# One unit's similarities two images ahead, behind the cluster sums, in a clustering and convolution kernel

## The chip, the cores and the metric

The kernel runs on one core of one Trainium2 chip. The metric is the device time of one execution in microseconds (us). The engines are named TensorE (PE), its weight loads (PEld), VectorE (DVE), ScalarE (ACT), GpSimd (POOL) and SyncE (SP), which issues the transfers.

## What is computed

Input x is 8 images of 512 channels by 32 x 48 pixels, float32; there are 40 centroids and a 512 x 512 weight matrix.

```python
xn = x / jnp.maximum(jnp.linalg.norm(x, axis=1, keepdims=True), EPS)
cn = centroids / jnp.maximum(jnp.linalg.norm(centroids, axis=1, keepdims=True), EPS)
sim = jnp.einsum('bchw,nc->bnhw', xn, cn)
idx = jnp.argmax(sim, axis=1)
onehot = jax.nn.one_hot(idx, N, dtype=x.dtype)
sum_x = jnp.einsum('bhwn,bchw->bnc', onehot, x)
count = jnp.sum(onehot, axis=(1, 2))
centroids_local = sum_x / jnp.maximum(count, 1.0)[..., None]
gathered = centroids_local[jnp.arange(B)[:, None, None], idx]
delta = jnp.transpose(gathered, (0, 3, 1, 2)) - x
alpha = jnp.exp(-jnp.mean(delta * delta, axis=1, keepdims=True))
y = x + alpha * delta
out = jnp.einsum('oc,bchw->bohw', W, y) + b[None, :, None, None]
return jax.nn.relu(out)
```

The pixel's own norm doesn't change its argmax, so the kernel leaves it out.

## The kernel before

**Units and slots.** An image has 1536 pixels, cut into three units of 512; unit g is part g % 3 of image g // 3, and there are 24. Channels lie on partitions in 4 chunks of 128. The order of all work is written out by hand, one list for each engine; engines meet at semaphores only. From unit 3 on the lists are loops over g, and I call one turn of the loop a slot. A slot holds two strands:

- *The unit itself.* TensorE's `gather(g, h)` multiplies the one-hot by the image's centroid means G, two of the four chunks for each half h, into the PSUM tile `gat`. VectorE's `delta` subtracts x into Z; ScalarE's `square` and VectorE's `add_squares` (three adds), ScalarE's `move_upper`, VectorE's `fold`, ScalarE's `high_sum` and VectorE's `low_sum` make the squared length in two parts, which TensorE's `sum_squares` adds over partitions into `al`. In the slot behind it ScalarE makes `exp`, VectorE `scale`s Z by it, GpSimd's `y_half` adds x, ScalarE's `high_half` rounds y to its high part YH and GpSimd's `low_half` makes the rest YL. Two slots after its gather (LAG = 2) comes `convolve(g, o)`: for each of four output groups o, 12 matmuls (4 chunks x YH, YL with the high weights and YH with the low ones) into one of two banks of `main`, then ScalarE's `relu`. A group waits until the relu two groups before it has emptied its bank, and group 0 waits for the halves of YL as it comes to them.
- *The next image.* Its similarities (`similarities`, L846, output tile 64 rows wide, two side by side) stand behind `gather(g, 1)`: units 0 and 1 in the first slot of an image, unit 2 in the second. ScalarE's `copy_sims` takes them out; `transpose_sims`, then VectorE's `best_sims` and `first_best` make the one-hot in the second slot. In the third slot `sum_clusters` (L891, also 64 rows wide) sums x by cluster for all three units, then `gather(g, 1)` and one convolution group follow, then `add_halves` (L901, L902), for which ScalarE's `copy_sums` and VectorE's `low_clusters` come first; `scale_means`, `high_means`, `rest_of_mean` and `parts_of_mean` (L449) make G for the gathers of the next slot. `count_onehot` counts the pixels of a cluster on ScalarE and writes a copy into `simS`.

**Pixels on partitions.** `sum_clusters` needs x turned. SyncE loads each unit a second time in blocks, and VectorE's `transpose_half` (L393) turns it into XT, two halves a unit; units 4 and 5 are turned by TensorE (`turn`) and copied by ScalarE (`keep_turned`). From unit 7 on, the first two units of an image are split in three bf16 parts: GpSimd's `first_rest` (L354, 2048 elements) and VectorE's `second_rest` (L401, 2048 elements, both of its inputs in SBUF) make the rests in XR.

**x itself** has two buffers. `load_x(g)` waits until `y_half` of unit g - 6 is made.

**The queue of a slot's end.** In slot order VectorE's list ends with `second_rest(g + 3)` in an image's first and second slot. GpSimd's list is, for each unit, `y_half` twice, `low_half` twice, then `first_rest` if a unit is due.

**Before the loop** the units 0 to 2 have lists of their own. There GpSimd's `add_chunks` (L362, L365) adds the squares of a unit in three adds, in place of the steps above, `sum_squares_direct` (L938) sums them, and unit 0's first two convolution groups are made in passes (`high_passes`, then L1058 with the low half of y).

Of the kernel before, what the change touches and what calls it, by code (L numbers as in the profile page):

```python
# [14 lines left out]
P = 128  # L15
# [14 lines left out]
NK = P  # L30
# [9 lines left out]

TURNED = (PARTS + 1, PARTS + 2)

# [6 lines left out]
def y_on_vector(g, h):  # L49

    return g == 0 or (g == 1 or g >= TAIL) and h == 1

# [42 lines left out]
def build(nc, x, cent, w, bias, out):  # L95
# [3 lines left out]
    with ctx:  # L99
# [58 lines left out]
        simP = [fa[:, 0, 0:256], fa[:, 1, 0:256], fa[:, 0, 256:512]]  # L158
# [53 lines left out]
        def squares(g, h):  # L212
            if g < DIRECT:

                return (OUT[0][:, :, :], OUT[1][:, :, :], XR[:, 0, :, :])[g][:, pair(h), :]
            return SQ[:, :, :] if h == 0 else gat[:, :, :]

# [95 lines left out]
        def _(pool):  # L313
# [66 lines left out]
        def _(dve):  # L380
# [71 lines left out]
            def delta(g, h):  # L452
                dve.wait_ge(gat_done, 2 * g + h + 1)
                if g >= 2:
                    wait_low(dve, g - 2, h)
                v_.tensor_tensor(Z[g % 2][:, pair(h), :], banks(g, h)[:, :, :],  # L456
                                 X[g // PARTS % 2][:, pair(h), span(g)], ALU.subtract).then_inc(z_done, 1)

# [95 lines left out]
            parts_of_mean(1)  # L554
            transpose_half(6, 0)
            low_half(1, 1)
            transpose_half(6, 1)
            for g in range(PARTS, UNITS):
                b, p = divmod(g, PARTS)
                beside = b + 1 < BATCH  # L560
                delta(g, 0)
                scale(g - 1, 0)
                scale(g - 1, 1)
                delta(g, 1)
# [3 lines left out]
                if beside and p == 2:  # L568
                    low_clusters(b + 1)
# [28 lines left out]
        def _(act):  # L598
# [7 lines left out]
            def keep_turned(g, half):  # L606

                done = PARTS * 2 + 2 * TURNED.index(g) + half + 1
                act.wait_ge(xp_done, done)
                a_.activation(XT[:, g % PARTS, HALF * half:HALF * (half + 1), :], (gat, main)[half][:, :, :],  # L610
                              ACT.Copy).then_inc(xe_act, 1)
# [501 lines left out]
```

## Time and profile before

| what | us |
|---|---|
| median of 3 runs | 414.45 |
| lowest, highest | 414.08, 415.33 |
| the profiled execution's own time | 414.81 |
| its span (first to last instruction) | 413.0 |
| TensorE busy | 405.5 |
| VectorE busy | 330.2 |
| ScalarE busy | 258.1 |
| GpSimd busy | 267.8 |

All rows come from one profiled execution. Starts are us from the span's start. A row with x2 merges two instructions.
### The profile page before, as it was taken

The numbers are of one execution on the slowest core, as the hardware profiler recorded it, in microseconds if no ns is written. First come the engines' busy times: TensorE is split into PE (matmuls) and PEld (weight loads), VectorE is DVE, ScalarE is ACT, GpSimd is POOL, SyncE is SP. The second block draws the span as 40 slices with busy tenths as digits, with TensorE's granted clock in tenths as the row PEclk, the third lists the DMA queues.
The fourth block names the chain that finished last, engine by engine and source line by source line (L and its number), as shares of the span: only waits on it lengthen the run. The fifth ranks groups of instructions, "written<-read, shape, count | busy, mean of one in ns | idle before, by whom it ended". The sixth has DMA issues, their size and how long they took to land.

```text
span 413.0 us, 5757 instructions
## 1 busy us (share of the span) xinstructions
PE 405.5 (98%) x2080; PEld 289.5 (70%) x2085; DVE 330.2 (80%) x404; ACT 258.1 (62%) x354; POOL 267.8 (65%) x120
## 2 busy tenths in 40 slices
PE   9999999999999999999999999999999999999996
PEld 6746475875777767775867757776777758777885
DVE  2438986689889889899798888898798996898730
ACT  6566773766674775665855676656846657576542
POOL 2003886993699666993879946996769937433420
PEclk9999999999999999999999999999999999999999
DMA  7992497767589395966979575993966240222223
GB/s 263 374 243 54 94 250 202 195 214 144 201 231 280 102 252 164 273 168 178 267 183 237 192 160 188 255 252 119 254 158 220 104 140 2 102 102 103 102 81 124
DMA packets 77823, 74.59 MB, mean 181 GB/s; under 512 B 13716, under 2 KB 52628, under 8 KB 77796
## 3 DMA queue, kind: packets, MB, share of 16 engines
q1 hardware_dynamic: 77796, 74.23, 64.7%
q8 instruction: 17, 0.28, 0.3%
q14 instruction: 10, 0.08, 0.1%
HBM read 46.30 MB, written 25.17 MB: 173 GB/s over the span
## 4 chain that ended last, share of the span: by engine, by line
PE 91%; POOL 4%; ACT 2%; DVE 1%; issue 1%; ACTq 0%; POOLq 0%
PE main L949 21%; PE main L950 20%; PE main L951 20%; PE fa L846 10%; PE sump L891 8%; PE gat L927 5%; POOL yl L347 2%; PE fa L855 1%; PE al L933 1%; PE al L984 1%; POOL xr L362 1%; PE main L964 1%; POOL o L362 1%; PE gat L964 1%; POOL o L365 1%; PE main L1058 1%
## 5 line engine op out<-in xcount | busy, mean ns | idle before, releaser
L949 PE MATMUL main<-yh,wh 128*128 128x512 f32 x376 | 153.3, 408 | 0.0
L950 PE MATMUL main<-yl,wh 128*128 128x512 f32 x376 | 146.7, 390 | 0.0
L951 PE MATMUL main<-yh,wl 128*128 128x512 f32 x376 | 146.6, 390 | 0.0
L340 POOL TENSOR_TENSOR z<-z,x 128x1024 f32<-128x1024 f32 x41 | 98.6, 2424 | 63.9 <-DVE z L480 63.9
L347 POOL TENSOR_TENSOR yl<-z,yh 128x1024 fp32r<-128x1024 f32 x43 | 103.8, 2434 | 9.1 <-ACT yh L639 9.1
L647 ACT ACTIVATE o<-main,bcol 128x512 f32<-128x512 f32 x96 | 65.6, 684 | 61.3 <-PE main L951 60.5
L949 PEld LDWEIGHTS main<-yh,wh 128*128 128x128 f32 x376 | 70.6, 188 | 21.3 <-issue 4.6
L951 PEld LDWEIGHTS main<-yh,wl 128*128 128x128 f32 x376 | 70.6, 188 | 15.1
L950 PEld LDWEIGHTS main<-yl,wh 128*128 128x128 f32 x376 | 70.7, 188 | 14.0
L354 POOL TENSOR_TENSOR xr<-xt 128x2048 f32<-128x2048 f32 x11 | 51.5, 4682 | 18.2 <-DVE xt L393 18.2
L456 DVE TENSOR_TENSOR z<-gat,x 128x1024 f32<-128x1024 f32 x46 | 56.0, 1218 | 6.8 <-PE gat L927 6.6
L480 DVE TENSOR_TENSOR z<-z,al 128x1024 f32<-128x1024 f32 x48 | 56.3, 1214 | 3.9 <-ACT al L634 3.9
L639 ACT ACTIVATE yh<-z 128x1024 fp32r<-128x1024 f32 x48 | 50.6, 1053 | 4.5 <-POOL z L340 2.9
L846 PE MATMUL fa<-x,c_t 128*64 128x256 f32 x384 | 46.9, 394 | 0.0
L393 DVE STREAM_TRANSPOSE xt<-xs 128x1024 f32<-128x1024 f32 x38 | 46.4, 1230 | 0.0
L846 PEld LDWEIGHTS fa<-x,c_t 128*64 128x64 f32 x384 | 26.6, 140 | 18.4 <-issue 7.0
L621 ACT ACTIVATE sq<-z 128x1024 f32<-128x1024 f32 x21 | 22.3, 1061 | 26.9 <-DVE z L456 26.9
L401 DVE TENSOR_TENSOR xr<-xr 128x2048 bf16<-128x2048 f32 x11 | 36.0, 3275 | 0.2
L621 ACT ACTIVATE gat<-z 128x1024 f32<-128x1024 f32 x21 | 21.5, 1024 | 21.3 <-DVE z L456 21.3
L891 PE MATMUL sump<-xt,oh 128*64 128x512 f32 (+1 forms) x148 | 31.7, 537 | 0.0
L362 POOL TENSOR_TENSOR o<-o 128x512 f32<-128x512 f32 x4 | 5.1, 1284 | 36.2 <-ACT o L621 36.2
L927 PE MATMUL gat<-oht,g 128*128 128x512 bf16 x87 | 26.7, 384 | 0.8 <-DVE g L449 0.4
(130 smaller groups left out, 394.2 us busy)
## 6 DMA issues: line engine op xcount, KB each, us to landing
out<-o SPq DMA_DIRECT2D x23, 1024.0 KB, 6.3
x<-x SPq DMA_DIRECT2D x21, 1024.0 KB, 5.5
xs<-x SPq DMA_DIRECT2D x76, 256.0 KB, 5.4
x<-x SPq DMA_DIRECT2D x12, 256.0 KB, 5.1
o<-w SPq DMA_DIRECT2D x1, 1024.0 KB, 8.9
out<-o SPq DMA_DIRECT2D x4, 256.0 KB, 2.0
sq<-centroids SPq DMA_DIRECT2D x2, 80.0 KB
oht<-oh SPq DMA_TRANSPOSE x7, 3.7
```

The costliest lines, as they stand in the source:

```text
L340: pool.tensor_tensor(z, z, X[g // PARTS % 2][:, pair(h), span(g)], ALU.add).then_inc(y_pool, 1)
L347: pool.tensor_tensor(YL[g % 2][:, pair(h), :], Z[g % 2][:, pair(h), :], YH[g % 2][:, pair(h), :].bitcast(F32), ALU.subtract).then_inc(lo_p ...
L354: pool.tensor_tensor(XR[:, g % PARTS, :, :].rearrange("p t c -> p (t c)"), xt.rearrange("p t c -> p (t c)"), halfword(xt, 1), ALU.subtract ...
L456: v_.tensor_tensor(Z[g % 2][:, pair(h), :], banks(g, h)[:, :, :], X[g // PARTS % 2][:, pair(h), span(g)], ALU.subtract).then_inc(z_done, 1)
L480: v_.tensor_tensor(z, z, al[:, :].unsqueeze(1).to_broadcast([P, 2, UNIT]), ALU.mult).then_inc(za_done, 1)
L639: a_.activation(YH[g % 2][:, pair(h), :], Z[g % 2][:, pair(h), :], ACT.Copy).then_inc(hi_done, 1)
L647: a_.activation(OUT[g % 2][:, o, :], main[:, o % 2, :], ACT.Relu, bias=bcol[:, o:o + 1]).then_inc(relu_done, 1)
L846: last = t_.matmul(simP[u][NPAD * h:NPAD * (h + 1), :], cT[:, k, :], toks, start=(k == 0), stop=(k == KC - 1))
L891: last = t_.matmul(sumP[NPAD * h:NPAD * (h + 1), :], onehot[:, slot(u, tile), :], x_part[:, tile * C:(tile + 1) * C], start=(opens and t = ...
L949: t_.matmul(main[:, o % 2, :], WH[:, k, rows], YH[g % 2][:, k, :], start=(k == 0), stop=False)
L950: t_.matmul(main[:, o % 2, :], WH[:, k, rows], YL[g % 2][:, k, :], start=False, stop=False)
L951: last = t_.matmul(main[:, o % 2, :], WL[:, k, rows], YH[g % 2][:, k, :], start=False, stop=(k == KC - 1))
```

## The change

1. From image 3 on, one unit's similarities are made two images ahead: in the third slot of an image b, directly behind the cluster sums of image b + 1, come those of unit 0 of image b + 2. The other two units' follow together in the second slot. The places of the three in PSUM are exchanged so that unit 0's does not lie where the mean is made. This holds in the slots of units 5, 8, 11, 14 and 17 (`late_group`); the slot of unit 20 stays as it was.
2. In those slots `add_halves` goes ahead of `gather(g, 1)`, and the slot's last convolution group and `sum_squares(g)` go behind the first gather of the next slot. ScalarE's copies, means and relus are put in an order that goes with it.
3. VectorE: in those slots `low_clusters` comes after the scaling, a transposed half on either side of `delta(g, 1)`, G before `low_sum`, and `second_rest(g + 4)` at the end, which stood in the next slot. `second_rest` is two instructions of 1024 instead of one of 2048.
4. GpSimd: for the unit handled in those slots `first_rest` goes ahead of the two `low_half`.
5. At the start: one tile of unit 4 is turned ahead of the similarities; the squares of unit 2 are added by VectorE; the low passes of unit 0 are made half by half; unit 6's second transposed half goes into slot 3.
6. `count_onehot` writes in place.

The list of SyncE, with all transfers, is the same in both kernels.

TensorE, the slot of unit 8, from its first gather. Before (L933 is the sum of squares of unit 7, L891 the cluster sums):

```order
L933 MATMUL al<-shl,ones 128x512
L927 MATMUL gat<-oht,g 128x512 x2
L891 MATMUL sump<-xt,oh 64x512 x6
...
L891 MATMUL sump<-xr,oh 64x512 x4
L927 MATMUL gat<-oht,g 128x512 x2
L949 MATMUL main<-yh,wh 128x512
```

And after (L953 the cluster sums, L908 similarities, L963 and L964 `add_halves`, L991 `gather`):

```order
L991 MATMUL gat<-oht,g 128x512 x2
L953 MATMUL sump<-xt,oh 64x512 x6
...
L953 MATMUL sump<-xr,oh 64x512 x4
L908 MATMUL fa<-x,c_t 64x256 x8
L963 MATMUL fa<-sums_h,select 128x512
L964 MATMUL fa<-sums_l,select 128x512
L991 MATMUL gat<-oht,g 128x512 x2
L1013 MATMUL main<-yh,wh 128x512
```

One unit's similarities and the two matmuls of `add_halves` now stand between the sums and the second gather.

VectorE, the slot of unit 8, from `low_clusters` (L435) to the next slot's first `delta` (L456). Before (L393 is the transpose, L474 `low_sum`, L449 G):

```order
L435 TENSOR_TENSOR sums_l<-sump,sums_h 128x512
L428 TENSOR_SCALAR cols<-cols 128x1
...
L466 TENSOR_TENSOR al<-sq,gat 128x512
L470 TENSOR_TENSOR al<-upper_sum,al 64x512
L441 SCALAR_TENSOR_TENSOR fa<-part,cols,fa 128x512
L444 CAST part<-fa 128x512
L474 TENSOR_TENSOR shl<-al,shl 64x512
L449 SCALAR_TENSOR_TENSOR g<-part,cols,fa 128x512
L393 STREAM_TRANSPOSE xt<-xs 128x8x4x32 x2
L456 TENSOR_TENSOR z<-gat,x 128x1024
```

And after (L456 is now `low_clusters`, L414 the transpose, L477 `delta`, L504 `low_sum`, L422 `second_rest`):

```order
L456 TENSOR_TENSOR sums_l<-sump,sums_h 128x512
L414 STREAM_TRANSPOSE xt<-xs 128x8x4x32
L477 TENSOR_TENSOR z<-gat,x 128x1024
...
L414 STREAM_TRANSPOSE xt<-xs 128x8x4x32
...
L500 TENSOR_TENSOR al<-upper_sum,al 64x512
L470 SCALAR_TENSOR_TENSOR g<-part,cols,fa 128x512
L504 TENSOR_TENSOR shl<-al,shl 64x512
L422 TENSOR_TENSOR xr<-xr 128x1024 x2
L477 TENSOR_TENSOR z<-gat,x 128x1024
```

The transposes moved up, and the two halves of `second_rest` now stand between `low_sum` and the next slot's `delta`.

GpSimd, the units 7 and 8 (worked on in the slots of units 8 and 9). Before (L340 `y_half`, L347 `low_half`, L354 `first_rest`):

```order
L340 TENSOR_TENSOR z<-z,x 128x1024 x2
L347 TENSOR_TENSOR yl<-z,yh 128x1024 x2
L354 TENSOR_TENSOR xr<-xt 128x2048
L340 TENSOR_TENSOR z<-z,x 128x1024 x2
L347 TENSOR_TENSOR yl<-z,yh 128x1024 x2
L354 TENSOR_TENSOR xr<-xt 128x2048
```

And after (L360, L367, L374 are the same three):

```order
L360 TENSOR_TENSOR z<-z,x 128x1024 x2
L374 TENSOR_TENSOR xr<-xt 128x2048
L367 TENSOR_TENSOR yl<-z,yh 128x1024 x2
L360 TENSOR_TENSOR z<-z,x 128x1024 x2
L367 TENSOR_TENSOR yl<-z,yh 128x1024 x2
L374 TENSOR_TENSOR xr<-xt 128x2048
```

In the slot of unit 8 `first_rest` moved ahead of the low halves; in the next it stayed.

The diff, cut to its core:

```diff
+def late_group(g):
+    return g >= PARTS and g % PARTS == 2 and g // PARTS + 2 < BATCH
+def units_compared(g):
+    if g < 2 * PARTS:
+        return ((0, 1), (2,), ())[g % PARTS]
+    return ((), (1, 2), ())[g % PARTS]
...
-        simP = [fa[:, 0, 0:256], fa[:, 1, 0:256], fa[:, 0, 256:512]]
+        simP = [fa[:, 1, 0:256], fa[:, 0, 0:256], fa[:, 1, 256:512]]
...
             for g in range(UNITS):
                 y_half(g, 0)
                 y_half(g, 1)
+                rest = g + 5 < UNITS and split(g + 5)
+                if rest and g % PARTS == 1:
+                    first_rest(g + 5)
                 low_half(g, 0)
                 low_half(g, 1)
-                if g == 1:
-                    add_chunks(2)
-                if g + 5 < UNITS and split(g + 5):
+                if rest and g % PARTS != 1:
                     first_rest(g + 5)
...
-            def second_rest(g):
+            def second_rest(g, h):
...
-                xr = XR[:, g % PARTS, :, :]
+                xr = XR[:, g % PARTS, HALF * h:HALF * (h + 1), :]
...
             parts_of_mean(1)
+            add_chunks(2, 0)
+            low_half(1, 1)
+            add_chunks(2, 1)
             transpose_half(6, 0)
-            low_half(1, 1)
-            transpose_half(6, 1)
             for g in range(PARTS, UNITS):
                 delta(g, 0)
+                if g == PARTS:
+                    transpose_half(g + 3, 1)
                 scale(g - 1, 0)
                 scale(g - 1, 1)
+                if late_group(g):
+                    low_clusters(b + 1)
+                    transpose_half(g + 4, 0)
                 delta(g, 1)
...
+                if late_group(g):
+                    transpose_half(g + 4, 1)
                 add_squares(g)
...
+                if late_group(g):
+                    rest_of_mean(b + 1)
                 fold(g)
-                if beside and p == 2:
+                if late_group(g):
+                    parts_of_mean(b + 1)
+                elif beside and p == 2:
                     rest_of_mean(b + 1)
...
                 if beside and p == 2:
-                    parts_of_mean(b + 1)
-                    if g + 4 < UNITS:
-                        transpose_half(g + 4, 0)
-                        transpose_half(g + 4, 1)
-                if g + 3 < UNITS and split(g + 3):
-                    second_rest(g + 3)
+                    if late_group(g):
+                        if split(g + 4):
+                            second_rest(g + 4, 0)
+                            second_rest(g + 4, 1)
+                    else:
+                        parts_of_mean(b + 1)
+                if p == 1 and g + 3 < UNITS and split(g + 3):
+                    second_rest(g + 3, 0)
+                    second_rest(g + 3, 1)
...
                 if g > PARTS:
-                    relu(g - 3, 3)
+                    if not late_group(g - 1):
+                        relu(g - 3, 3)
                     exp(g - 1)
                 square(g, 0)
+                if late_group(g - 1):
+                    relu(g - 3, 3)
                 if beside and p == 2:
                     copy_sums(b + 1)
+                    if late_group(g):
+                        copy_sims(3 * b + 6)
                     count_onehot(b + 1)
                     high_half(g - 1, 0)
                     square(g, 1)
...
             add_halves(1)
-            wait_low(pe, 0, 0)
-            wait_low(pe, 0, 1)
-            for o in range(2):
-                for k in range(KC):
+            for h in range(2):
+                wait_low(pe, 0, h)
+                for o in range(2):
+                    for k in (2 * h, 2 * h + 1):
...
             for g in range(PARTS, UNITS):
                 gather(g, 0)
+                if late_group(g - 1):
+                    sum_squares(g - 1)
+                    convolve(g - 1 - LAG, 3)
                 if beside and p == 2:
                     for u in sum_order(b + 1):
                         sum_clusters(b + 1, u)
+                    if late_group(g):
+                        similarities(3 * b + 6)
+                        add_halves(b + 1)
                     gather(g, 1)
                     convolve(g - LAG, 0)
-                    add_halves(b + 1)
+                    if not late_group(g):
+                        add_halves(b + 1)
...
-                convolve(g - LAG, 3)
-                sum_squares(g)
+                if not late_group(g):
+                    convolve(g - LAG, 3)
+                    sum_squares(g)
```

## Rows read from the trace of the kernel before

**Rows 1.** The page's first part: busy time, share of the span, instructions.
```profile
PE 405.5 (98%) x2080; PEld 289.5 (70%) x2085; DVE 330.2 (80%) x404; ACT 258.1 (62%) x354; POOL 267.8 (65%) x120
```

**Rows 2.** What TensorE waited for: total us, times, longest.
```profile
PE al L938 <- POOL xr L365: 0.9, 1, 0.9
PE main L1058 <- POOL yl L347: 0.6, 1, 0.6
PE gat L927 <- DVE g L449: 0.4, 1, 0.4
```

**Rows 3.** The chain that ended last, two images: start us, us, what.
```profile
207.84 0.23 PE al L933
...
259.60 3.60 PE fa L846 x32
263.21 0.43 PE main L949
...
275.47 1.88 PE fa L846 x16
...
286.66 0.45 PE gat L927 x2
287.10 4.58 PE sump L891 x32
291.69 0.54 PE gat L927 x2
294.96 0.24 PE fa L901
...
303.62 0.23 PE al L933
```

**Rows 4.** VectorE in order of time, slot of unit 14: start us, us, instruction.
```profile
242.39 2.35 DVE L480 TENSOR_TENSOR z<-z,al 128x1024 f32<-128x1024 f32 x2
244.65 1.22 DVE L456 TENSOR_TENSOR z<-gat,x 128x1024 f32<-128x1024 f32 x1
...
248.13 0.69 DVE L462 TENSOR_TENSOR sq<-sq,gat 128x512 f32<-128x512 f32 x1 [1.41 <-ACT gat L621]
...
254.38 2.36 DVE L393 STREAM_TRANSPOSE xt<-xs 128x1024 f32<-128x1024 f32 x2
```

**Rows 5.** All engines in order of time, images 0 and 1.
```profile
58.79 2.42 POOL L347 TENSOR_TENSOR yl<-z,yh 128x1024 fp32r<-128x1024 f32 x1 [1.60 <-ACT yh L639]
...
59.23 0.75 DVE L449 SCALAR_TENSOR_TENSOR g<-part,cols,fa 128x512 bf16<-128x512 bf16 x1
...
67.08 0.59 PE L927 MATMUL gat<-oht,g 128*128 128x512 bf16 x2
```

**Rows 6.** The page's part 6: x loads, KB each, median us to landing.
```profile
x<-x SPq DMA_DIRECT2D x21, 1024.0 KB, 5.5
```

**Rows 7.** ScalarE in order of time, slot of unit 14.
```profile
244.33 1.48 ACT L680 ACTIVATE sims<-oht 128x1536 bf16<-128x1536 bf16 x1
...
246.13 1.06 ACT L639 ACTIVATE yh<-z 128x1024 fp32r<-128x1024 f32 x1 [0.23 <-POOL z L340]
```

**Rows 8.** The instructions of line 354, first_rest: ns min/median/max.
```profile
L354 POOL TENSOR_TENSOR xr<-xt x11: 3602/3605/5988, 79.2 to 317.7; 128x2048 f32<-128x2048 f32 x11
```

**Rows 9.** VectorE and GpSimd in order of time, slot of unit 15.
```profile
265.07 4.75 POOL L347 TENSOR_TENSOR yl<-z,yh 128x1024 fp32r<-128x1024 f32 x2
...
268.15 4.18 DVE L401 TENSOR_TENSOR xr<-xr 128x2048 bf16<-128x2048 f32 x1
...
269.79 5.96 POOL L354 TENSOR_TENSOR xr<-xt 128x2048 f32<-128x2048 f32 x1
```

**Rows 10.** The instructions of line 401, second_rest: ns min/median/max.
```profile
L401 DVE TENSOR_TENSOR xr<-xr x11: 2551/2602/4186, 94.8 to 334.6; 128x2048 bf16<-128x2048 f32 x11
```

**Rows 11.** VectorE and GpSimd in order of time, tail.
```profile
390.19 2.40 POOL L340 TENSOR_TENSOR z<-z,x 128x1024 f32<-128x1024 f32 x1 [4.73 <-DVE z L480]
...
391.28 2.40 DVE L488 TENSOR_TENSOR z<-z,x 128x1024 f32<-128x1024 f32 x1
```

More of the change, by code:

```diff
@@ L457, in delta, with add_chunks @@
                                  X[g // PARTS % 2][:, pair(h), span(g)], ALU.subtract).then_inc(z_done, 1)
+            def add_chunks(g, h):
+                sq = squares(g, h)
+                dve.wait_ge(sq_done, 2 * g + h + 1)
+                v_.tensor_tensor(sq[:, 0, :], sq[:, 0, :], sq[:, 1, :], ALU.add).then_inc(two_done, 1)
+                if h == 1:
+                    dve.wait_ge(two_done, 2 * g + 2)
+                    first_two = squares(g, 0)[:, 0, :]
+                    v_.tensor_tensor(first_two, first_two, sq[:, 0, :], ALU.add).then_inc(four_done, 1)
             def add_squares(g):
@@ L604, in keep_transposed, with keep_turned @@
                               ACT.Copy).then_inc(xe_act, 1)
[L606 to L611, printed above, removed]
+            def keep_turned(step):
+                g, tiles = TURNS[step]
+                act.wait_ge(xp_done, PARTS * 2 + step + 1)
+                a_.activation(XT[:, g % PARTS, tiles[0]:tiles[-1] + 1, :], turn_bank(tiles), ACT.Copy
+                              ).then_inc(xe_act, 1)
             def square(g, h):
@@ L788, in _ @@
                     if beside:
-                        copy_sims(3 * b + 3 + 2 * p)
+                        for u in units_compared(g)[0:1]:
+                            copy_sims(3 * b + 3 + u)
                     high_half(g - 1, 0)
+                    if beside:
+                        for u in units_compared(g)[1:]:
+                            copy_sims(3 * b + 3 + u)
+                    if not beside:
+                        relu(g - 2, 1)
                     if beside and p == 0:
-                        copy_sims(3 * b + 4)
-                    if not beside:
                         relu(g - 2, 1)
@@ L966, in transpose_x, with turn @@
                 last.then_inc(xp_done, 1)
-            def turn(g, half):
-                if g == TURNED[0]:
-                    pe.wait_ge(z_done, 1 + half)
-                else:
-                    pe.wait_ge(xe_act, 6 + half)
-                for t in range(HALF):
-                    at = g % PARTS * UNIT + (HALF * half + t) * P
+            def turn(step):
+                g, tiles = TURNS[step]
+                if step == 0:
+                    pe.wait_ge(wl_done, 1)
+                elif step < 3:
+                    pe.wait_ge(z_done, step)
+                else:
+                    pe.wait_ge(xe_act, KEPT + step - 1)
+                for i, t in enumerate(tiles):
+                    at = g % PARTS * UNIT + t * P
                     for k in range(KC):
-                        last = t_.transpose((gat, main)[half][:, t, k * P:(k + 1) * P], X[1][:, k, at:at + P],
+                        last = t_.transpose(turn_bank(tiles)[:, i, k * P:(k + 1) * P], X[1][:, k, at:at + P],
                                             ident[:, :])
@@ L1028, in _ @@
             transpose_weights(3)
+            pe.wait_ge(x_in[1][1], 16)
+            turn(0)
             similarities(3)
@@ L1053, in _ @@
             add_halves(1)
-            wait_low(pe, 0, 0)
-            wait_low(pe, 0, 1)
-            for o in range(2):
-                for k in range(KC):
-                    last = t_.matmul(main[:, o, :], WH[:, k, o * P:(o + 1) * P], YL[0][:, k, :],
-                                     start=False, stop=(k == KC - 1))
-                last.then_inc(main_done, 1)
+            for h in range(2):
+                wait_low(pe, 0, h)
+                for o in range(2):
+                    for k in (2 * h, 2 * h + 1):
+                        last = t_.matmul(main[:, o, :], WH[:, k, o * P:(o + 1) * P], YL[0][:, k, :],
+                                         start=False, stop=(k == KC - 1))
+                    if h == 1:
+                        last.then_inc(main_done, 1)
             gather(2, 1)
```

72 lines of the change are left out of this document (42 added, 30 removed).

## The prediction

> **What bounds the kernel now.** The page's first part comes first: TensorE is busy for 405.5 of 413.0 us [rows 1]. The list of what TensorE waited for says the rest: its waits are all in the first 67 us, the largest 0.9, 0.6 and 0.4 us, and none comes after [rows 2]. From there on it streams one matmul of 512 columns every 0.23 us, and one image takes three slots, 47.9 us (two images between the sums of squares at 207.84 and 303.62 [rows 3]). So a change can win only what lies between unlike matmuls, and those early waits; it can lose as soon as an operand comes late. The time goes by one execution, 414.81 us around a span of 413.0; the median of the runs is 414.45, 0.36 less. About 0.3% (1.2 us) is what a measurement of this kernel can tell from no change.
>
> **Joined sims.** TensorE's instructions stay the same. In the chain, sims of two units take 3.60 us (32 records) and those of one 1.88 (16), so 16 records cost 1.72 and the block 0.16 more; the first convolution behind a block takes 0.43 us instead of 0.23 [rows 3]. Entering and leaving the half-width tile thus costs 0.36 us for a block. The cluster sums, half-width too, pay the entry and 0.09 on the way out (the two gathers behind them take 0.54 instead of 0.45 [rows 3]): 0.25. Before, an image has three such blocks; afterwards the single unit's sims stand directly behind the sums, one entry and one exit for both. Saved: 0.25 + 0.36 - 0.36 = **0.25 us**, at best the whole 0.36, in five slots (units 5, 8, 11, 14, 17, which I call late slots): 1.25 us, upper end 1.8. The Trainium skill (TensorEngine Tiling, Key Properties) says that a change of tiling mode drains the engine; the 0.20 us on the first convolution agrees.
>
> **The start.** Two things are removed. The last eight matmuls of unit 0 wait 0.6 us for GpSimd's second low half, 54.0 us [rows 2]; now four of them need the first half alone and fill the wait, so the gather behind comes about 1.0 us earlier. And GpSimd's sums of unit 2's squares, for which TensorE waits 0.9 [rows 2], go to VectorE as three adds (0.69 each, as the add at 248.13 [rows 4]). But VectorE must then do, ahead of delta(3,0): first add, low half (1.2), two more adds, one transpose (1.2). Its G is ready at 59.98 before [rows 5], 58.8 now, but GpSimd's low half (58.79 + 2.42 before [rows 5], 0.6 earlier now, to 60.6) holds off an add with two SBUF inputs (shown below). So: 60.6 + 0.6 + 1.2 + 0.6 + 0.7 + 1.2 + 1.2 = 66.1, and gather(3,1), which waits for delta(3,0), starts at 66.3 against 67.08 [rows 5]: **0.8 us** gained. If GpSimd held nothing off, 1.9 (2.0 upper end); if the adds come later than I think, 0. Turning one tile earlier fills a wait of 0.4 us for G [rows 2] and is given back in the chain of squares and GpSimd adds that follows: 0. The count written in place, the fetches (their order is unchanged) and the swapped relus are priced at nothing: TensorE runs over them.
> The x block of the early unit is asked for when y is made, in the slot before; it lands in 5.5 us [rows 6], and by the step times below y ends some 5 us before that slot's end and the sims begin 5 us into the next: hidden, and it would cost its lateness if not.
>
> **The late slot, step by step.** Zero is its gather(g,0). TensorE: gather 0.45, sums 4.58, sims 1.72 + 0.20, halves 0.46, gather(g,1) from 7.4 to 7.9, 36 convolution matmuls 8.2 (from the first halves matmul at 294.96 to the sum of squares at 303.62, 8.66, less 0.46 [rows 3]): end at **16.0**. Then gather 0.46, sum 0.23, the moved group 2.73: convolve(g-1) begins at 19.4, needs its second low half at **20.8**, and gather(g+1,1), which needs delta(g+1,0), is due at **22.2**.
> VectorE: scales until about 5.9 (2.35 for two [rows 4]), low_clusters to 6.5 while the sims run to 6.9, so the halves don't wait. delta(g,1) 8.0 to 9.2 (1.22 [rows 4]); counts; second transpose half 9.4 to 10.6 (2.36 for two [rows 4]). ScalarE counts from 7.35 (1.48), makes the high half (1.06) [rows 7] and the square from 9.8 to 10.8; VectorE's three adds end at 12.8, two steps of the mean, the fold and G, about 0.7 each like the adds, at 14.2, 14.9 and 15.5 (due 16.0: no wait), low_sum 16.2 (due 16.5: 0.3 spare). At 16.1 it asks for the first half of second_rest.
> GpSimd: y 5.0 to 9.8, first_rest (3.60 [rows 8]) when the transpose is done, 10.7 to 14.3, low halves (4.75 for two [rows 9]) to 16.7 and 19.1. Without disturbance that is 1.7 ahead of 20.8.
> **The disturbance.** second_rest takes 2.55 us at least and 4.19 at most [rows 10]. In the slow ones it began 1.67 us before GpSimd's low halves ended (265.07 + 4.75 = 269.82, against 268.15) and took 1.6 longer; then GpSimd's first_rest took 5.96 instead of 3.60, 2.4 longer, about as long as second_rest still ran [rows 8 to 10]. In the tail an add of VectorE that takes 1.2 elsewhere takes 2.40, starting 1.3 us before GpSimd's y ends [rows 11]. So here such instructions, two SBUF inputs on each side, exclude each other, and the one that waits gets in at the next boundary. In the late slot second_rest now meets the low halves, with little left to the deadline. Half 0 (1.3) waits for low 0, 16.7 to 18.0. What comes next no row shows: VectorE's half 1 or the waiting low 1.
> **Forecast case:** half 1 follows at once, to 19.3, and low 1 runs 19.3 to 21.7, 0.9 us past 20.8. TensorE waits **0.9 us** (0.5 to 1.3, since a dozen steps precede it) in each of five slots: 4.5. delta(g+1,0) ends at 20.4, in time. Sum: 414.81 - 0.8 - 1.25 + 4.5 = 417.3; less 0.36, **416.9**. With 0.5 to 1.3: 414.9 to 418.9.
>
> **Rival 1, slower still: GpSimd goes between the halves.** low 1 runs 18.0 to 20.4, in time, but half 1 ends at 21.7 and delta(g+1,0) at 22.8, past 22.2. ScalarE does square(g+1,0) ahead of relu(g-2,3) (new order), so that relu ends at 24.5, and the convolution group that needs its bank, due at 22.7, starts at 24.6: 1.9 us in each late slot, 9.5 in all, **421.9**. For it: at 269.8 the one that had waited got in. Against it: that one was VectorE, which may simply come first. The Trainium skill (SBUF: State Buffer, Who interferes with whom) says the instruction that issues first gets the shared port for all its length and the other blocks; the long rows agree, and by issue order low 1, queued at 16.7, would go ahead of half 1: this rival.
> **Rival 2, faster: the stall is not there.** If low 1 is done by 20.8, TensorE never waits in the late slots. It decides if the four lengths (3.6, 2.4, 1.3, 2.4) start 0.9 us sooner than 10.7, or 20.8 comes as much later, or the second halves slip behind low 1 at no cost (there are 1.7 us of slack without the disturbance, and delta(g+1,0) has 1.8 even then). The profile before has the same collision in an image's first slot, 2.4 us of it on GpSimd [rows 8, 9], and TensorE did not notice. Then 414.81 - 2.05 = 412.8, less 0.36: **412.4**, down to 411 with the upper ends.
> **Rival 3, nothing:** sims behind the sums pay a switch all the same (another operand type), and the start gives back its 0.8: 414.5.
>
> **Numbers.** Forecast case 0.42, of which 0.11 falls within 0.3% (stall near 0.4) and 0.31 above; rival 1 0.18, slower; rival 2 0.34, faster; rival 3 0.06, same. Faster 0.34, same 0.17, slower 0.49. The range goes from 411.5, inside rival 2, to 422.0, about the middle of rival 1; it leaves out some 0.15.
>
> **What would show it.** Joined sims: in the chain, sums x32 followed by sims x16 with no longer first record, and no 0.54 gather. Start: gather(3,1) near 66.3, no wait for a GpSimd add at 66. Forecast case: waits "PE main <- POOL yl", five of 0.9 us, with second_rest halves of 1.9 and 1.3 us and one low half of about 5. Rival 1: halves of 1.9 and 3.7 us, waits of the gather for VectorE's z and of main for a relu. Rival 2: no waits of TensorE past 67 us. The prediction is wrong if period and waits of the late slots fit none of these, above all if the halves find GpSimd idle.

## The result, and the profile after

The changed kernel takes 416.25 us (median of 7 runs, 415.8 to 417.25), and the kernel before took 414.67 beside it (413.86 to 415.36). The ratio is 1.0041, with a 95% interval of 1.0023 to 1.0060: slower by 0.4%.

The first part of the page answers to [rows 1], and two groups of its fifth part to the lines whose places moved (`low_half` is L367, `second_rest` L422):

```profile
PE 404.7 (98%) x2085; PEld 288.2 (70%) x2085; DVE 329.0 (79%) x418; ACT 257.8 (62%) x355; POOL 263.4 (64%) x117
...
L367 POOL TENSOR_TENSOR yl<-z,yh 128x1024 fp32r<-128x1024 f32 x43 | 115.7, 2704 | 13.1 <-ACT yh L685 13.0
...
L422 DVE TENSOR_TENSOR xr<-xr 128x1024 bf16<-128x1024 f32 x22 | 30.5, 1442 | 0.2
```

TensorE is busy 0.8 us less, and yet the span is 414.0 us instead of 413.0. What TensorE waited for, in the answer that stands against [rows 2] (total us, times, longest):

```profile
PE main L1013 <- POOL yl L367: 3.1, 5, 0.6
...
PE gat L991 <- DVE z L477: 0.8, 1, 0.8
PE al L963 <- DVE sums_l L456: 0.3, 1, 0.3
```

The two waits of the start, for GpSimd's adds (0.9) and for its low half (0.6), are gone, and so is the gather's 0.4 for G. New at the start is the gather's 0.8 for unit 3's `delta`. New behind it are five waits for the low half of y, one in each late slot. The list puts 0.6 us on each; the stream shows what each costs in full. TensorE in order of time, the end of the slot of unit 14 (start us, us, instruction, idle before):

```profile
254.74 0.55 PE L997 MATMUL al<-shl,ones 128*128 128x512 f32 x1
255.13 0.40 PE L1013 MATMUL main<-yh,wh 128*128 128x512 f32 x1
...
260.00 0.47 PE L1013 MATMUL main<-yh,wh 128*128 128x512 f32 x1 [0.61 <-POOL yl L367]
...
261.44 0.60 PE L991 MATMUL gat<-oht,g 128*128 128x512 bf16 x2
```

From 255.13 to 261.44 are 6.31 us for 24 matmuls. One matmul of the stream takes 0.227 us (the 17 steps from 255.13 to 258.99), so 24 would take 5.45 and the stall costs 0.86. (In a stream the matmul at 260.00 would have begun at 259.22.)

**The same by periods.** Each image has one block of cluster sums, and the starts of these blocks on TensorE's timeline cut the program into pieces that can be laid side by side. A piece is named by the images whose sums it lies between:

| piece, us | before | after | difference |
|---|---|---|---|
| from the turning of the centroids, at 3.4 us, to image 0 | 17.02 | 16.15 | -0.87 |
| image 0 to 1 | 21.49 | 21.21 | -0.28 |
| 1 to 2 | 53.18 | 52.30 | -0.88 |
| 2 to 3 (first late slot) | 48.26 | 48.88 | +0.62 |
| the next four, each | 47.88 to 47.89 | 48.47 to 48.52 | +0.58 to +0.63 |
| last block to the end | 78.08 | 78.09 | 0 |

The first piece hangs on when the first x arrives and not on the change: in the profiled runs below, whose code there is the same as the changed kernel's, it is between 16.1 and 19.4 us. The longest is e3's, where TensorE's weight loads for the first similarities wait 0.70 and 1.20 us for the x loads; its profiled execution took 418.27 us, 2.8 over that kernel's median. Without the first piece the change wins 1.16 us at the start and loses 3.0 in five late slots: 1.85 us in all, against 1.58 between the medians.

### The profile page after: what moved, and what is told of

It is laid out like the page before. It is cut to its first block, busy times and chain, and to the rows that moved or that the text cites. A ratio compares the mean times of both kernels' runs of the same rounds, so it can differ in the third digit from the quotient of the medians.

```text
span 414.0 us, 5776 instructions
## 1 busy us (share of the span) xinstructions
PE 404.7 (98%) x2085; PEld 288.2 (70%) x2085; DVE 329.0 (79%) x418; ACT 257.8 (62%) x355; POOL 263.4 (64%) x117
## 4 chain that ended last, share of the span: by engine, by line
PE 58%; POOL 16%; DVE 14%; issue 9%; ACT 1%; DMA 1%; SPq 0%; POOLq 0%; ACTq 0%; DVEq 0%
PE main L1013 13%; PE main L1014 12%; PE main L1015 12%; POOL yl L367 9%; PE fa L908 8%; POOL z L360 6%; PE gat L991 3%; DVE z L477 2%; PE sump L953 2%; DVE xt L414 2%; DVE z L510 2%; DVE xr L422 2%; PE fa L917 1%; DMA x<-x 1%; PE main L1075 1%
## 5 line engine op out<-in xcount | busy, mean ns | idle before, releaser
L360 POOL TENSOR_TENSOR z<-z,x 128x1024 f32<-128x1024 f32 x41 | 98.4, 2418 | 77.1 <-DVE z L510 76.7
L367 POOL TENSOR_TENSOR yl<-z,yh 128x1024 fp32r<-128x1024 f32 x43 | 115.7, 2704 | 13.1 <-ACT yh L685 13.0
L477 DVE TENSOR_TENSOR z<-gat,x 128x1024 f32<-128x1024 f32 x46 | 56.1, 1220 | 20.0 <-PE gat L991 20.0
L414 DVE STREAM_TRANSPOSE xt<-xs 128x1024 f32<-128x1024 f32 x38 | 46.9, 1234 | 0.0
L908 PE MATMUL fa<-x,c_t 128*64 128x256 f32 x384 | 45.8, 383 | 0.2 <-DMA x<-x 0.2
L374 POOL TENSOR_TENSOR xr<-xt 128x2048 f32<-128x2048 f32 x11 | 39.6, 3599 | 7.5 <-DVE xt L414 7.5
L908 PEld LDWEIGHTS fa<-x,c_t 128*64 128x64 f32 x384 | 26.0, 136 | 18.0 <-issue 4.0
L667 ACT ACTIVATE gat<-z 128x1024 f32<-128x1024 f32 x21 | 21.5, 1025 | 19.6 <-DVE z L477 19.6
L953 PE MATMUL sump<-xt,oh 128*64 128x512 f32 (+1 forms) x148 | 31.7, 537 | 0.0
L422 DVE TENSOR_TENSOR xr<-xr 128x1024 bf16<-128x1024 f32 x22 | 30.5, 1442 | 0.2
L991 PE MATMUL gat<-oht,g 128*128 128x512 bf16 x92 | 27.8, 384 | 0.8 <-DVE z L477 0.8
```

The lines of the kernel that those rows point to most:

```text
L360: pool.tensor_tensor(z, z, X[g // PARTS % 2][:, pair(h), span(g)], ALU.add).then_inc(y_pool, 1)
L367: pool.tensor_tensor(YL[g % 2][:, pair(h), :], Z[g % 2][:, pair(h), :], YH[g % 2][:, pair(h), :].bitcast(F32), ALU.subtract).then_inc(lo_p ...
L414: last = v_.transpose(XT[:, g % PARTS, :, :].rearrange("p t (m j) -> p m t j", j=BLK)[:, blocks, :, :], XS[g % 2][:, blocks, :])
L667: a_.activation(squares(g, h), Z[g % 2][:, pair(h), :], ACT.Square).then_inc(sq_done, 1)
L908: last = t_.matmul(simP[u][NPAD * h:NPAD * (h + 1), :], cT[:, k, :], toks, start=(k == 0), stop=(k == KC - 1))
```

## The experiments

Two theories stood after the result. **The port theory**: in the late slot VectorE's two halves of `second_rest`, each with two inputs in SBUF, run one behind the other, and GpSimd's second `low_half`, which has waited since half 0 got in, gets in only behind both. **The length rival**: the late slot simply holds too much, on GpSimd (`first_rest` is now ahead of the low halves) or on VectorE, and the collision only shows up where the slack was gone anyhow. All ratios are to the kernel before on the same chip; the period is that of the steady images.

**e1, `second_rest` in one piece again.**

```diff
-                            second_rest(g + 4, 0)
-                            second_rest(g + 4, 1)
+                            second_rest(g + 4)
```

> second_rest in one instruction of 2048 again, wherever it stands; all else as changed. Theory (VectorE's two halves keep GpSimd out for their whole 2.6 us, so the split does nothing): time stays within 0.3 us of the changed kernel's 416.25, in each late slot TensorE waits 0.6 us for a low half and that low half lasts 4.8 us. Rival (the split lets something of GpSimd in and saves a part): the wait grows by up to 1.3 us in each of five slots, 418 to 422 us.

Measured: 416.58 us, 1.0049 [1.0035, 1.0062]; the five waits for yl are the same 3.1 us, period 48.5. VectorE and GpSimd in order of time, slot of unit 14:

```profile
254.78 2.99 DVE L422 TENSOR_TENSOR xr<-xr 128x2048 bf16<-128x2048 f32 x1
...
252.87 7.13 POOL L367 TENSOR_TENSOR yl<-z,yh 128x1024 fp32r<-128x1024 f32 x2
```

And the same place in the changed kernel, where the cut is:

```profile
254.62 3.01 DVE L422 TENSOR_TENSOR xr<-xr 128x1024 bf16<-128x1024 f32 x2
...
252.71 7.14 POOL L367 TENSOR_TENSOR yl<-z,yh 128x1024 fp32r<-128x1024 f32 x2
```

One piece or two, GpSimd's pair takes 7.13 or 7.14 us, 2.4 more than its 4.75 [rows 9]. The cut lets nobody in. This fits the port theory, and it doesn't speak against the length rival.

**e2, half 1 behind the next slot's scaling.**

```diff
                 scale(g - 1, 1)
+                if late_group(g - 1) and split(g + 3):
+                    second_rest(g + 3, 1)
...
-                            second_rest(g + 4, 1)
```

> The second half of second_rest in a late slot stands behind the two scale instructions of the next slot, the first stays at the slot's end. Theory (the port is what makes the low half late): GpSimd's second low half begins as soon as the first half of second_rest is over, is held off 1.3 us instead of 2.6, and ends before it is needed; no wait of TensorE for a low half, each of five periods 0.8 us shorter, 416.25 - 3.9 = 412.4 us. Rival (first_rest ahead of the low halves is too much for GpSimd, port or not): the wait stays at 0.6 us, 416 us. Second rival (the half now meets y in the next slot and makes delta late): a new wait for z or a longer slot, 414 to 416 us.

Measured: 415.16 us, 1.0012 [1.0004, 1.0021]; period 48.25. The waits for yl are gone, and what TensorE waited for has a new first line:

```profile
PE al L998 <- DVE shl L504: 2.0, 5, 0.4
```

VectorE and GpSimd, slot of unit 14 and the start of the next:

```profile
254.68 1.75 DVE L422 TENSOR_TENSOR xr<-xr 128x1024 bf16<-128x1024 f32 x1
256.32 1.21 DVE L477 TENSOR_TENSOR z<-gat,x 128x1024 f32<-128x1024 f32 x1
...
259.70 2.68 DVE L422 TENSOR_TENSOR xr<-xr 128x1024 bf16<-128x1024 f32 x1
...
252.77 5.89 POOL L367 TENSOR_TENSOR yl<-z,yh 128x1024 fp32r<-128x1024 f32 x2
258.73 5.88 POOL L360 TENSOR_TENSOR z<-z,x 128x1024 f32<-128x1024 f32 x2
```

With half 1 out of the way GpSimd's pair takes 5.89, the 4.75 and one half of 1.1 to 1.3 us. The `delta` that follows half 0 has one input in PSUM and doesn't hold GpSimd off. So the first stall is cured by moving one instruction of VectorE alone, with nothing shorter on GpSimd. But half 1 now meets `y_half`, waits for it (2.68 instead of 1.33), and makes everything of VectorE behind it late, up to `low_sum`, for which TensorE waits 0.4.

**e3, both halves back at the next slot's end**, where `second_rest` stood before:

```diff
-                    if late_group(g):
-                        if split(g + 4):
-                            second_rest(g + 4, 0)
-                            second_rest(g + 4, 1)
-                    else:
+                    if not late_group(g):
                         parts_of_mean(b + 1)
-                if p == 1 and g + 3 < UNITS and split(g + 3):
+                if g + 3 < UNITS and split(g + 3):
```

> Both halves of second_rest go back to the end of the next slot, where they stood before; all else as changed. Theory: the wait for a low half in the late slot goes (0.8 us in each of five), but in the next slot the halves meet a low half and hold first_rest, VectorE is free some 2 us later, and delta of the slot behind it ends after its second gather is due: a wait of 0.5 to 1 us for z in its place, 412.5 to 416.5 us. Rival (GpSimd's order alone): 416 us with the old wait.

Measured: 415.51 us, 1.0032 [1.0017, 1.0046]; period 48.35. No wait for yl, but a wait of the gather behind the sums of squares in each image. What TensorE waited for, and VectorE and GpSimd at the end of the slot of unit 15:

```profile
PE gat L987 <- DVE z L477: 3.8, 6, 0.9
```

```profile
271.45 3.48 DVE L422 TENSOR_TENSOR xr<-xr 128x1024 bf16<-128x1024 f32 x2
274.81 1.22 DVE L477 TENSOR_TENSOR z<-gat,x 128x1024 f32<-128x1024 f32 x1
...
270.01 2.40 POOL L367 TENSOR_TENSOR yl<-z,yh 128x1024 fp32r<-128x1024 f32 x1 [0.25 <-ACT yh L681]
272.37 5.98 POOL L374 TENSOR_TENSOR xr<-xt 128x2048 f32<-128x2048 f32 x1
```

Half 0 waits 0.97 us for GpSimd's low half to end (270.01 + 2.40 = 272.41), both halves then run back to back, `delta` is late and TensorE's gather at 276.17 waits 0.60. GpSimd's `first_rest`, which would have begun at 272.4, takes 5.98 instead of 3.60 and so gets in behind both. It is the collision of [rows 9], in the same slot as there, and here it costs because the next slot begins earlier than it did before: its first gather comes 30.5 us after the cluster sums instead of 32.5.

**e8, as e3, and `low_half` ahead of `first_rest` for every unit.**

```diff
-                if rest and g % PARTS == 1:
-                    first_rest(g + 5)
                 low_half(g, 0)
                 low_half(g, 1)
-                if rest and g % PARTS != 1:
+                if rest:
                     first_rest(g + 5)
```

> The changed kernel with GpSimd's first_rest behind the low halves in every slot, and both halves of second_rest at the next slot's end, as before the change. Theory: the low halves meet no second_rest and are in time; but first_rest ends 3.6 us into the next slot and makes y and the next low halves late, and both halves of second_rest then hold GpSimd: some wait of up to 0.9 us a period for z or a low half, 412.5 to 416 us. Rival (the order low halves, then first_rest is free): no wait, 412.4 us, as good as the kernel with the split halves.

Measured: 415.9 us, 1.0035 [1.0023, 1.0046]; period 48.35 and the same waits, 3.8 us in six. GpSimd's order makes no difference to e3. This speaks against the length rival on GpSimd: with `first_rest` behind, the low halves end at 254.8, 5 us sooner than in the changed kernel, and nothing is won.

**e9, the late halves with one input in PSUM.** Where the changed kernel subtracts two SBUF tensors, this one takes its second input from the PSUM tile of the cluster sums. Place, size and output of the instruction stay, and its second input alone differs. The third bf16 part of x for the units 9, 12, 15, 18 and 21 is thereby left out of the sums. The run was made after e5, whose period its expectation takes over.

```diff
+                v_.tensor_tensor(halfword(xr, 0).rearrange("p (a c) -> p a c", a=2), xr,
+                                 sumP[:, :].unsqueeze(1).to_broadcast([P, 2, UNIT]), ALU.subtract
...
-                            second_rest(g + 4, 0)
-                            second_rest(g + 4, 1)
+                            like_rest(g + 4, 0)
+                            like_rest(g + 4, 1)
```

> The changed kernel with every instruction in its place; only in the late slots the two halves of second_rest take their second input from PSUM (the cluster sums' tile) instead of SBUF, same sizes and types. So the third bf16 part of the units 9, 12, 15, 18 and 21 is left out and something else is in its place. Theory (two SBUF inputs on each side exclude each other): the halves start at once and take 1.3 us each, the low halves 2.4 each, no wait of TensorE for a low half, period 47.6 us, 412.3 us. Rival (VectorE's work at that moment, or GpSimd's order, makes the low half late without any port): the wait of 0.6 us and the period of 48.47 stay, 416.2 us.

Measured: 412.28 us, 0.9945 [0.993, 0.996]; period 47.60, no wait of TensorE for yl. VectorE and GpSimd, slot of unit 14:

```profile
253.11 2.63 DVE L428 TENSOR_TENSOR xr<-xr,sump 128x1024 bf16<-128x1024 f32 x2
...
251.20 4.77 POOL L367 TENSOR_TENSOR yl<-z,yh 128x1024 fp32r<-128x1024 f32 x2
```

The order and the sizes are the same, and both engines now run side by side without holding each other up: 2.63 instead of 3.01 us on VectorE, 4.77 instead of 7.14 on GpSimd. This decides for the port theory. The whole stall, 48.47 - 47.60 = 0.87 us a period, is the exclusion, and the slot holds nothing too long otherwise. The Trainium skill (SBUF — State Buffer, Who interferes with whom) puts the exclusion on a port that the two engines share; by these rows the input in PSUM lifts it.

**e5, half 0 where it is, half 1 at the end of the next slot's list**, behind `low_sum`:

```diff
                             second_rest(g + 4, 0)
-                            second_rest(g + 4, 1)
                     else:
                         parts_of_mean(b + 1)
+                if late_group(g - 1) and split(g + 3):
+                    second_rest(g + 3, 1)
```

> As the kernel with the second half moved, but it stands at the end of the next slot, behind low_sum, where VectorE waited 1.1 us for the gather behind it. Theory (port, and in the last kernel the half merely made delta and so low_sum 0.6 us late): low_sum is early again, low halves are in time, no wait of TensorE in the late slot nor behind it; the half meets a low half, waits for it and ends before that slot's first delta is due; period 48.47 - 0.8 = 47.7 us, time 416.25 - 3.9 = 412.4 us. Rival (VectorE has no room left in any slot): a wait for z or for low_sum of 0.4 to 0.9 us appears again, 414.5 to 416 us.

Measured: **412.31 us**, 0.994 [0.9925, 0.9955] (the kernel before: 414.25 beside it); period 47.60. It computes the same as the changed kernel and beats both. TensorE has no wait behind the start. VectorE and GpSimd, slots of units 14 and 15:

```profile
253.16 1.74 DVE L422 TENSOR_TENSOR xr<-xr 128x1024 bf16<-128x1024 f32 x1
254.79 1.20 DVE L477 TENSOR_TENSOR z<-gat,x 128x1024 f32<-128x1024 f32 x1
...
267.20 2.20 DVE L422 TENSOR_TENSOR xr<-xr 128x1024 bf16<-128x1024 f32 x1
...
251.24 5.89 POOL L367 TENSOR_TENSOR yl<-z,yh 128x1024 fp32r<-128x1024 f32 x2
...
268.11 4.72 POOL L374 TENSOR_TENSOR xr<-xt 128x2048 f32<-128x2048 f32 x1
```

Both halves still collide, each with one instruction of GpSimd, and each is held off by it (1.74 and 2.20 instead of 1.33). But each collision costs GpSimd only 1.1 us. The low halves end at 257.13 (251.24 + 5.89) and TensorE's matmul that needs them begins at 257.75, in the stream.

**e7, e5 with the joined sims pulled apart again**: they stand behind `gather(g, 1)`, with `add_halves`, and not directly behind the sums.

```diff
                     if late_group(g):
+                        gather(g, 1)
                         similarities(3 * b + 6)
                         add_halves(b + 1)
-                    gather(g, 1)
+                    else:
+                        gather(g, 1)
```

> On the kernel with the second half at the next slot's end: in the late slots the early unit's similarities stand behind gather(g, 1) instead of directly behind the cluster sums, so the full-width gather lies between the two half-width blocks. Theory (a change of tile width costs 0.25 to 0.36 us, which joining saves): the period is 0.2 to 0.36 us longer than in that kernel, 1 to 1.8 us in all. Rival (width changes cost nothing here, the gap belongs to weights or operand types): the same period. The gather comes 2 us earlier, which makes delta and all behind it earlier, so no new wait.

Measured: 414.96 us, 1.0013 [1.0000, 1.0026]; period 48.24, which is 0.64 more than e5 and more than the 0.36 that I had put as the upper end. TensorE in order of time, slot of unit 14:

```profile
243.50 0.60 PE L992 MATMUL gat<-oht,g 128*128 128x512 bf16 x2
244.03 1.95 PE L909 MATMUL fa<-x,c_t 128*64 128x256 f32 x16
245.91 0.50 PE L964 MATMUL fa<-sums_h,select 128*128 128x512 f32 x1
...
246.48 0.40 PE L1014 MATMUL main<-yh,wh 128*128 128x512 f32 x1
...
254.67 0.60 PE L992 MATMUL gat<-oht,g 128*128 128x512 bf16 x2
255.42 0.47 PE L998 MATMUL al<-shl,ones 128*128 128x512 f32 x1
```

From the start of the sums, 238.91, to the first convolution are 7.57 us, against 7.14 in e5 (237.45 to 244.59); the convolution's 36 matmuls take 8.19 there and 8.40 in e5, where the gather stands directly ahead of them. Together 15.76 against 15.54: the separation costs **0.22 us**. The other 0.4 is a new wait, which I had said would not be there. `add_halves` is 0.7 us later, and so is the rest of VectorE's list, down to `low_sum`:

```profile
254.58 0.69 DVE L504 TENSOR_TENSOR shl<-al,shl 64x512 fp32r<-64x512 f32 x1
```

It ends at 255.27, and the sum of squares that needs it begins at 255.42. From the gather at 254.67 to the first convolution behind it are 1.05 us (255.72), in e5 0.67 (252.99 to 253.66). The times of the periods thus hold the separation only together with this delay.

**e6, the start alone.** `late_group` is False, the units are compared as before and `first_rest` and the late transposes are where they were; the start and the cut of `second_rest` remain. ScalarE's relu in an image's first slot also stands as before.

```diff
-    return g >= PARTS and g % PARTS == 2 and g // PARTS + 2 < BATCH
+    return False
...
-    if g < 2 * PARTS:
-        return ((0, 1), (2,), ())[g % PARTS]
-    return ((), (1, 2), ())[g % PARTS]
+    return ((0, 1), (2,), ())[g % PARTS]
```

> The start of the change alone again, now with ScalarE's relu(g-2, 1) behind move_upper and the high half in an image's first slot, as before the change. Theory (in the last start-only kernel this relu, which waits for a convolution group, stood ahead of move_upper while 3.6 us of similarities still stood ahead of that group, and so made fold, low_sum, second_rest and the one-hot late, 0.9 us a period): period 47.9 us again, only the start's 1.2 us gained, 413.4 us. Rival (halving second_rest or moving a transpose costs the 0.9): period 48.8, 418 us.

Measured: 413.40 us, 0.9973 [0.9962, 0.9984]; periods 21.20, 52.30 and then 47.88. The start is worth what its two pieces say (0.29 and 0.88 us), and as the steady period is that of before, the cut of `second_rest` and the count in place cost and bring nothing there.

**e4, the same with the relu order of the changed kernel** (`relu(g - 2, 1)` ahead of `high_half(g - 1, 1)` in an image's first slot). It was the first try at the start alone; e6 differs from it in this order only:

```diff
-                    if g == PARTS:
+                    if beside and p == 0:
                         relu(g - 2, 1)
...
-                    if beside and p == 0 and g > PARTS:
-                        relu(g - 2, 1)
```

> Only the start of the change, with second_rest in halves: no unit's similarities are moved, all slots from unit 3 on as before. Theory: the turned tile 0.3 us, the low passes by halves and the squares on VectorE 0.8 us, 1.1 us less than before, 413.5 us, and no wait of TensorE for GpSimd's adds at 66 us. If the extra 0.85 us by which the changed kernel's first sums came earlier in its profile belong to it too: 412.7. Rival (the start is hidden again later): same as before, 414.6.

Measured: 418.08 us, 1.0089 [1.0074, 1.0103], 4.6 us off what I expected. The period is 48.82 instead of 47.88, so one relu in another place costs 0.94 us an image. ScalarE in order of time, first slot of image 4:

```profile
215.81 0.46 ACT L703 ACTIVATE sims<-fa,cstat 128x256 f32<-128x256 f32 x1
218.17 0.69 ACT L692 ACTIVATE o<-main,bcol 128x512 f32<-128x512 f32 x1 [1.90 <-PE main L1014]
218.88 0.59 ACT L670 ACTIVATE upper_sum<-al 64x512 f32<-64x512 f32 x1
219.38 1.05 ACT L684 ACTIVATE yh<-z 128x1024 fp32r<-128x1024 f32 x1
```

The relu waits 1.90 us for its convolution group, because two units' sims stand ahead of that group on TensorE, and `move_upper` and `high_half` queue behind the relu. TensorE feels it in the two slots behind, in each of five images:

```profile
PE sump L952 <- DVE xt L410: 1.6, 5, 0.3
PE main L1012 <- ACT o L692: 1.0, 5, 0.2
```

Laid beside e6, a period loses 0.38 us where the cluster sums wait for turned x, and 0.56 in the stretch in which a convolution group waits for a relu. In the changed kernel no sims are in the first slot, the group is done sooner, and the order is harmless. So the order has a price only without the moved similarities.

**e10, e6 with the squares of unit 2 added by GpSimd again.**

```diff
+                if g == 1:
+                    add_chunks(2)
...
-            add_chunks(2, 0)
             low_half(1, 1)
-            add_chunks(2, 1)
```

> The clean start-only kernel (413.4 us) with the adds of unit 2's squares back on GpSimd; the low passes by halves and the turned tile stay. Theory of the prediction (both parts are needed: with the low passes early the next gate is TensorE's wait for those adds, which follow GpSimd's low half): the wait for GpSimd's adds at 65 us returns and grows, from the cluster sums of image 1 to those of image 2 it takes 52.6 to 53.0 us instead of 52.3, time 413.7 to 414.1 us. Rival (the low passes alone give it all): 52.3 us, 413.4.

Measured: 413.89 us, 0.9981 [0.9971, 0.9991]; the piece from image 1 to 2 is 52.75 instead of 52.30, and the wait for GpSimd's add is back with 1.2 us. So of the 0.88 us the passes by halves bring 0.43 and VectorE's adds 0.45. The wait for the add grows from 0.9 to 1.2 us when only the passes change, which takes part of their gain back.

## Why the prediction was right

The forecast was 416.9 us against 416.25 measured, and 2.45 us over the kernel before where 1.58 (by medians) or 1.85 (by periods) were measured. The likeliest case happened as described, and two terms of its sum were somewhat off, both on the side of the start: its 0.8 measured 0.88, and a term priced at 0 measured 0.28.

**The late slot's timeline held to 0.2 us.** With 238.38, the first gather, as zero:

| step | forecast | measured |
|---|---|---|
| slot end (next gather) | 16.0 | 16.1 |
| `first_rest` | 10.7 to 14.3 | 10.8 to 14.4 |
| `second_rest` asked for | 16.1 | 16.2 |
| low half 0 ends | 16.7 | 16.7 |
| half 1 of `second_rest` ends | 19.3 | 19.3 |
| low half 1 ends | 21.7 | 21.5 |
| TensorE's loss | 0.9 | 0.87 |

**Who goes next.** That was the open point, and no row of before showed it: the prediction gave its case 0.42 and put the rivals at 421.9, 412.4 and 414.5 us. That the time came out within 0.7 us rests on this choice having been the right one, which was a likely guess and not a derivation. The chain of the changed kernel, its second low half in the slot of unit 14 by itself, and the instructions of line 422 (ns min/median/max) show the forecast case:

```profile
301.18 7.15 POOL yl L367 x2
308.33 0.14 issue
308.47 0.47 PE main L1013
```

```profile
255.06 4.79 POOL L367 TENSOR_TENSOR yl<-z,yh 128x1024 fp32r<-128x1024 f32 x1
```

```profile
L422 DVE TENSOR_TENSOR xr<-xr x22: 1329/1364/1741, 92.8 to 336.2; 128x1024 bf16<-128x1024 f32 x22
```

No half takes more than 1.74 us, so none waits between two halves for a whole 2.4 us of GpSimd, which rival 1 needs (3.7). Low half 1 is the one that waits, from 255.1 to about 257.5 (its 4.79 us less the 2.4 of an undisturbed one). Rival 1 fell at that step: where VectorE's next instruction stood ready, it ran ahead of the GpSimd instruction that had waited for 1.3 us. The rule of the Trainium skill (SBUF — State Buffer, Who interferes with whom) on which it leaned, that the instruction that issues first gets the port, agrees here with one instruction against another: the first low half, already running, held half 0 off. Taken as the order in which instructions began to wait, it fails for low half 1, whose record starts at 255.06, ahead of half 1 at about 256.3. The trace doesn't show when half 1 issued, so why it goes first stays open. Rival 2 fell because nothing came 0.9 us sooner. Rival 2's time did appear, in e5 and e9 (412.31, 412.28 against 412.4), as soon as the stall was taken out by another way. Rival 3 fell with the saving.

**Joined sims: 0.25 forecast, 0.29 measured** (47.89 before, 47.60 in e5 and e9, which have them and no stall). That it is the joining, and not the rest of the reordered slot, is supported by e7's 0.22 for the separation alone, and by no more than that, since e7 moved `add_halves` too.

**The start: 0.8 forecast, 0.88 measured, and a term missed.** TensorE's gather waits for delta(3,0), as said, and GpSimd's low half holds off VectorE's first add, which takes 2.27 us instead of 0.69. Counted from the cluster sums of image 1, gather(3,1) begins at 24.28 us (65.07 - 40.79) against 25.15 before (67.08 - 41.93). GpSimd, VectorE and TensorE in the changed kernel's start:

```profile
57.24 2.41 POOL L367 TENSOR_TENSOR yl<-z,yh 128x1024 fp32r<-128x1024 f32 x1 [1.17 <-ACT yh L685]
...
57.92 2.27 DVE L483 TENSOR_TENSOR xr<-xr 128x512 f32<-128x512 f32 x1
60.12 1.22 DVE L525 TENSOR_TENSOR yl<-z,yh 128x1024 fp32r<-128x1024 f32 x1
...
65.07 0.59 PE L991 MATMUL gat<-oht,g 128*128 128x512 bf16 x2 [0.80 <-DVE z L477]
```

The mis-sized term is the turned tile, which the prediction priced at 0: it would fill the wait of 0.4 us for G and be given back in the chain of squares and GpSimd adds that follows. It is kept, for the most part: the piece from image 0 to 1 is 0.28 us shorter in the changed kernel and in e1 to e10 alike (21.20 to 21.21 against 21.49). TensorE around it, in the changed kernel:

```profile
27.44 0.60 PE L1046 MATMUL gat<-ident,x 128*128 128x128 f32 x4
27.97 3.67 PE L908 MATMUL fa<-x,c_t 128*64 128x256 f32 x32
31.58 0.61 PE L991 MATMUL gat<-oht,g 128*128 128x512 bf16 x2
```

The gather at 31.58 no longer waits, and the work that was pulled ahead is missing later, where TensorE was bound by its own work and not by GpSimd. This is read from the trace: no run puts the tile back and leaves the rest. The forecast of nothing for the rest of the change (x earlier, the count in place, the swapped relus) held inside it; e4 shows that for the relus that is so only beside the moved sims.

**The sum.** Forecast -0.8 - 1.25 + 4.5 = +2.45. Measured -1.16 - 5 x 0.29 + 5 x 0.87 = +1.74, and +1.85 by the periods themselves. The difference between the two is 0.02 us a period.

## What to carry to other kernels

When two engines exclude each other, add up the whole row of such instructions that stand back to back on one of them, and don't look at the length of each alone: two pieces back to back are as bad as one whole of their length, and a piece of another kind between them lets the other engine in. An order that saves time on the bound engine spends slack elsewhere, so look for what now meets what; here 1.5 us of saving was outweighed three times over by one instruction of 1.3 us in the wrong place, and moving that instruction (e5) kept the whole saving. And a reordering of one engine's list is only harmless beside the order of the others it was made for (e4), so test parts of a change with that in mind.

## What the runs showed of the hardware

- A GpSimd instruction that has waited through one VectorE instruction was not let in at the boundary to the next, where that next one stood ready and was of the same kind (two inputs in SBUF): in the changed kernel (7.14 us for two of 2.4) and in e3, where a `first_rest` of 3.60 took 5.98. Without the boundary, in e1, it takes as long (7.13). A VectorE instruction that waits did get in when GpSimd's current one ended, ahead of GpSimd's next, in all these runs.
- Taking one of the two inputs from PSUM removed the exclusion entirely (2.63 and 4.77 us side by side, e9), and VectorE's `delta`, which has such inputs, let GpSimd run (5.89, e2 and e5).
- The first 20 us vary with the arrival of the first x by about 3 us between executions (16.1 to 19.4 us from the turning of the centroids to the first cluster sums). That is more than the whole effect of this change, so the profiled executions could only be compared piece by piece.
